# Four decoder stages on one core: the first step of self-attention prepared inside cross-attention

## The reference

```python
x = layernorm(x + attn(x))     # gated linear recurrence: sigmoid gates, associative scan, rms norm
x = layernorm(x + xattn(x, ctx_2048))
x = layernorm(x + ffn(x))
```

```python
q = rmsnorm(x @ Wq.T); k = rmsnorm(context @ Wk.T); v = context @ Wv.T
out = softmax(q @ k.T * 16 ** -0.5) @ v
```

```python
h = rms(x, w_ln1)
q, k, v = h @ wq + bq, h @ wk + bk, h @ wv + bv
q, k = rope(q, k)
x = x + softmax(causal(q @ k.T * 32 ** -0.5)) @ v @ wo
h = rms(x, w_ln2)
x = x + routed(h) + shared(h)
```

## Time and profile before

| | |
|---|---|
| median of 3 runs | 2638.78 us (2637.13 to 2641.35) |
| profiled execution, its own time | 2640.4 us |
| its span | 2638.7 us |
| granted TensorE clock, mean | 0.972 |
| TensorE busy | 2423.2 us (92%) |
| VectorE, ScalarE, GpSimd busy | 1349.4, 1362.4, 903.0 us |
| instructions | 39037 |

### The profile page before, as it was taken

One profiled execution on the slowest core, in us unless ns is written; L12 is line 12 of the kernel. 1 busy time (PEld: TensorE's weight loads), 2 busy tenths in 40 slices (PEclk: granted clock), 3 DMA queues, 4 the chain that ended last, 5 costly groups with the idle time before them and its releaser, 6 DMA issues. The chain is left out here.

```text
span 2638.7 us, 39037 instructions
## 1 busy us (share of the span) xinstructions
PE 2423.2 (92%) x15376; PEld 1558.5 (59%) x15376; DVE 1349.4 (51%) x2098; ACT 1362.4 (52%) x1731; POOL 903.0 (34%) x589
## 2 busy tenths in 40 slices
PE   7996989999999999999995899998899999999997
PEld 5885644444444444444224565655578888888786
DVE  5566534434443434343005555555655566665775
ACT  4221467666776777667993443433422355555221
POOL 1224654555455536554003333332040111111220
PEclk9997999999999999999996999999999999999999
DMA  5002675576547573855426100001162366665330
GB/s 175 17 1 82 195 201 139 133 198 172 130 121 208 150 173 83 226 153 135 113 55 212 44 1 9 9 17 51 60 203 98 102 238 207 236 211 173 124 126 34
DMA packets 207429, 330.91 MB, mean 125 GB/s; under 512 B 70992, under 2 KB 125520, under 8 KB 207056
## 3 DMA queue, kind: packets, MB, share of 16 engines
q1 hardware_dynamic: 190032, 256.46, 34.4%
q0 software_dynamic: 15056, 68.03, 7.8%
q10 hardware_dynamic: 2160, 3.93, 0.5%
HBM read 241.00 MB, written 99.42 MB: 129 GB/s over the span
## 5 line engine op out<-in xcount | busy, mean ns | idle before, releaser
L880 ACT ACTIVATE A_c_prob<-c_psum 128x1024 f32<-128x1024 f32 x832 | 786.8, 1030 | 290.6 <-PE c_psum L1083 282.3
L826 POOL TENSOR_TENSOR c_rr<-c_ms,c_half 128x32 f32<-128x32 f32 (+1 forms) x72 | 372.5, 5177 | 436.5 <-DVE c_ms L897 436.5
L1092 PE MATMUL c_psum<-A_c_prob,c_vq 128*17 128x512 f32 x3328 | 419.0, 604 | 11.2 <-DVE c_oT L1003 9.7
L1083 PE MATMUL c_psum<-c_qq,c_kq 64*128 64x512 f32 x1664 | 293.3, 441 | 27.2 <-ACT A_c_prob L880 15.4
L134 PE MATMUL c_psum<-R_c_w,S_c_c 128*128 128x512 f32 x1248 | 314.3, 401 | 0.9 <-DVE S_c_t L960 0.5
L134 PEld LDWEIGHTS c_psum<-R_c_w,S_c_c 128*128 128x128 f32 x1248 | 228.4, 189 | 123.7 <-issue 43.1
L1083 PEld LDWEIGHTS c_psum<-c_qq,c_kq 64*128 64x128 f32 x1664 | 138.2, 186 | 186.7 <-ACT A_c_prob L880 107.7
L134 PE MATMUL m_psum<-R_m_t,m_up_hi 128*128 128x256 f32 (+1 forms) x1104 | 203.5, 285 | 23.9 <-DVE R_m_t L2241 23.9
L2286 PE MATMUL m_psum<-A_m_dn_hi,A_m_a 128*128 128x512 f32 (+1 forms) x628 | 206.3, 398 | 10.7 <-DVE A_m_a L2095 10.7
L937 DVE COPY c_raw<-c_psum 128x256 f32<-128x256 f32 x89 | 37.8, 425 | 332.2 <-PE c_psum L134 332.2
L1530 DVE TENSOR_REDUCE s_topx<-s_psum 128x4 f32<-128x2048 f32 (+1 forms) x64 | 95.5, 1493 | 178.1 <-PE s_psum L1642 178.1
(11 more groups left out here) (279 smaller groups left out, 4361.6 us busy)
## 6 DMA issues: line engine op xcount, KB each, us to landing
c_kq<-kd SPq DMA_DIRECT2D x248, 208.0 KB, 5.9
kd<-S_c_t SPq DMA_DIRECT2D x96, 256.0 KB, 3.5
A_c_raw<-in_ctxT SPq DMA_DIRECT2D x89, 256.0 KB, 4.8
qd<-A_c_q SPq DMA_DIRECT2D x64, 256.0 KB
c_qq<-qd SPq DMA_DIRECT2D x64, 256.0 KB, 3.2
vd<-c_vt SPq DMA_DIRECT2D x104, 136.0 KB, 3.0
c_vq<-vd SPq DMA_DIRECT2D x31, 442.0 KB, 9.2
R_m_hs<-slots SPq DMA_DIRECT2D x23, 512.0 KB, 7.4
```

Of the source, the lines that this page charges most:

```text
L826: pool.tensor_tensor(rr[:, unit % RB, 0:n], ms[:, unit % RB, 0:n], half[:, 0:n], ALU.pow).then_inc(s_r, 1)
L880: act.activation(prob[:, t % PB, 2 * (u % 2):2 * (u % 2) + 2, :], score_banks[u % 3], ACT.Exp, scale=XD ** -0.5).then_inc(s_ex, 1)
L1083: mm = pe.matmul(score_banks[u % 3][:, s, :], kq[rows, q % 2, u % 2, kt * P:(kt + 1) * P], qq[rows, q % 2, u % 2, :], start=True, stop=True)
L1092: mm = pe.matmul(o_bank[32 * j:32 * j + VW, :], vq[:, q % 2, kt, j, :], prob[:, t % PB, j, :], start=kt == 0, stop=kt == CT - 1)
```

## The change

A fourth region Q (2 units) is added. It takes cross-attention's `raw` and `c_raw`, later the query and key parts `qk_hi` and `qk_lo` of self-attention, and `dn_raw`, `dn_lo` and `work` of the experts' stage. Cross-attention's `vt` moves into region A, and its `on` into `sq`.

The planner gets twelve more items, H0 to H3 (turns of batch 0 for self-attention) and A0 to A7 (the four quarters of the query projection of step 0, then of the key projection, three matmuls each). They are placed in blocks with one weighted sum, not before 14 blocks after the last projection. By these rules they stand in blocks 243, 245, 247, 249 (H) and 251, 253, 255, 257, 259, 261, 263, 265 (A). While a projection is between its quarters no O may be placed: O28 moves from block 253 to 258 and O29 from 261 to 266.

In block 234 (`line.ahead`) SP issues the loads of wq, wk, wv, w1 and bqk, ahead of quad 28's loads in block 235; in block 244 cosine and sine. GpSimd casts the three weights to their high parts, VectorE squares the rows of batch 0, makes the low parts and scales the rows; VectorE and GpSimd also empty the H items and rotate and split step 0's queries and keys. ScalarE does nothing of it. Self-attention then starts with its five small loads, the load of wo and the slots, and with the first maxima; A(1,0), A(1,1), V0 and V1 are placed behind one of the four maxima each.

```diff
@@ class Timeline
+    QUARTERS = 4
+        later = [("H", i) for i in range(KC)] + [("A", i) for i in range(2 * self.QUARTERS)]
-            o_ready = quads and quads[0][1] <= k - 1
+            half_way = later and later[0][0] == "A" and later[0][1] % self.QUARTERS
+            o_ready = quads and quads[0][1] <= k - 1 and not half_way
+            elif later and not turns and not heavy and len(ready) < 2 and k >= max(unit_done.values()) + 14:
+                got = later.pop(0)
+        self.ahead = put_at["T", B * self.UPB - 1] + 2
@@ cross_attention, SP
+                if k == line.ahead:
+                    sp.wait_ge(s_put, last_turn.index + 1)
+                    for i in range(3):
+                        sp.wait_ge(s_vst[i], 16 * sum(1 for n in range(2 * B * CT) if v_buf(n) == i))
+                    for c in range(KC):
+                        sp.wait_ge(s_qst[c], 16 * 4 * B)
+                    for i, name in enumerate(("wq", "wk", "wv")):
+                        sp.dma_start(staged[i], d[name].rearrange("(k p) n -> p k n", p=P)).then_inc(s_stage[i], 16)
+                    sp.dma_start(w1[:], d["w1"]).then_inc(s_small, 16)
+                    sp.dma_start(bqk[:], d["bqk"]).then_inc(s_small, 16)
+                if k == line.ahead + 10:
+                    sp.wait_ge(s_slo, 3)
+                    sp.dma_start(cos, d["cos"]).then_inc(s_angle, 16)
+                    sp.dma_start(sin, d["sin"]).then_inc(s_angle, 16)
@@ cross_attention, GpSimd
+                if piece is last_turn:
+                    pool.wait_ge(s_put, last_products.index + 1)
+                    for i in range(3):
+                        pool.wait_ge(s_stage[i], 16)
+                        pool.tensor_copy(sw_hi[i], staged[i]).then_inc(s_shi, 1)
+                    pool.wait_ge(s_sms, 1)
+                    pool.tensor_tensor(srr[:], sms[:], half[:, 0:TT], ALU.pow).then_inc(s_srr, 1)
+                if piece.kind == "A" and piece.i % line.QUARTERS == line.QUARTERS - 1:
+                    i = piece.i // line.QUARTERS
+                    pool.wait_ge(s_angle, 32)
+                    pool.tensor_tensor(rot[:, i], qk[:, i], cos, ALU.mult).then_inc(s_cos, 1)
+                    pool.tensor_tensor(rot[:, i], rot[:, i], shuffled[:, i], ALU.add).then_inc(s_rot, 1)
+                    pool.tensor_copy(qk_hi[:, 0, i], rot[:, i]).then_inc(s_qkhi, 1)
+                    pool.tensor_tensor(qk_lo[:, 0, i], rot[:, i], qk_hi[:, 0, i], ALU.subtract).then_inc(s_qklo, 1)
...
@@ cross_attention, VectorE
+                    dve.wait_ge(s_xo, i + 1)
+                if piece.kind == "H":
+                    dve.wait_ge(s_small, 32)
+                    dve.tensor_scalar(h_hi[:, i, :], src[:], w1[:, i:i + 1], None, ALU.mult).then_inc(s_hhi, 1)
+                    dve.scalar_tensor_tensor(h_lo[:, i, :], src[:], w1[:, i:i + 1], h_hi[:, i, :], ALU.mult, ALU.subtract).then_inc(s_hlo, 1)
+                if piece.kind == "A" and i % line.QUARTERS == line.QUARTERS - 1:
+                    i //= line.QUARTERS
+                    dve.tensor_scalar(qk[:, i], src[:], bqk[:, i, 0:1], None, ALU.add).then_inc(s_qb, 1)
+                    dve.stream_shuffle(shuffled[:, i], qk[:, i], [(x + SD // 2) % SD for x in range(SD)]).then_inc(s_turned, 1)
+                    dve.tensor_tensor(shuffled[:, i], shuffled[:, i], sin, ALU.mult).then_inc(s_sin, 1)
...
+            def self_attention_ahead(j):
+                if 0 <= j < TT:
+                    own.done(dve.tensor_tensor(sq[:], X[:, j], X[:, j], ALU.mult))
+                    dve.tensor_reduce(ss[:, j:j + 1], sq[:], AX_X, ALU.add).then_inc(s_ss, 1)
+                if j == TT - 1:
+                    dve.tensor_scalar(sms[:], ss[:], 1.0 / H, 1e-6, ALU.mult, ALU.add).then_inc(s_sms, 1)
+                if 4 <= j < 7:
+                    dve.wait_ge(s_shi, j - 3)
+                    dve.tensor_tensor(sw_lo[j - 4], staged[j - 4], sw_hi[j - 4], ALU.subtract).then_inc(s_slo, 1)
+                if 7 <= j < 9:
+                    dve.wait_ge(s_srr, 1)
+                    for t in (2 * j - 14, 2 * j - 13):
+                        dve.tensor_scalar(xs[:, t], X[:, t], srr[:, t:t + 1], None, ALU.mult).then_inc(s_xs, 1)
...
+                self_attention_ahead(k - line.ahead)
@@ cross_attention, TensorE
+                if piece.kind == "H":
+                    pe.wait_ge(s_xs, TT)
+                    for t in range(TT):
+                        mm = pe.transpose(dst[:, t * P:(t + 1) * P], xs[:, t, i * P:(i + 1) * P], ident[:])
+                if piece.kind == "A":
+                    i, part = divmod(i, line.QUARTERS)
+                    pe.wait_ge(s_slo, i + 1)
+                    pe.wait_ge(s_hlo, KC)
+                    mm = product3(pe, dst[:], lambda _: sw_hi[i][:, part, 0:P], lambda _: sw_lo[i][:, part, 0:P],
+                                  lambda _: h_hi[:, part, :], lambda _: h_lo[:, part, :], 1, first=part == 0, last=part == KC - 1)
@@ class Steps
-        self.start = [self.item("H", 0, k) for k in range(KC)] + [self.item("A", n, i) for n in range(2) for i in range(2)]
+        self.start = [self.item("A", 1, i) for i in range(2)]
@@ self_attention, SP
-            for i in range(4):
-                if i == 3:
-                    sp.wait_ge(s_wlo, 3)
-                sp.dma_start(w_raw[i], d[names[i]].rearrange("(k p) n -> p k n", p=P)).then_inc(s_w[i], 16)
-                if i == 0:
-                    for dst, src in ((w1, "w1"), (bqk, "bqk"), (bv, "bv"), (cos, "cos"), (sin, "sin")):
-                        sp.dma_start(dst[:], d[src]).then_inc(s_ld, 16)
+            for dst, src in ((bqk, "bqk"), (sin, "sin"), (cos, "cos"), (w1, "w1"), (bv, "bv")):
+                sp.dma_start(dst[:], d[src]).then_inc(s_ld, 16)
+            sp.dma_start(wo_raw, d["wo"].rearrange("(k p) n -> p k n", p=P)).then_inc(s_w, 16)
@@ self_attention, VectorE
             dve.wait_ge(s_ld, 80)
...
             for t in reversed(range(TT)):
                 maximum(0, t)
-            low_weights(5)
+                if t >= 2:
+                    take(line.start[TT - 1 - t])
+            dve.wait_ge(s_whi, 1)
+            dve.tensor_tensor(w_lo[3], wo_raw, w_hi[3], ALU.subtract).then_inc(s_wlo, 1)
@@ self_attention, TensorE
-            for item in line.start:
-                put(item)
-            pe.wait_ge(s_hi, 2)
             for t in reversed(range(TT)):
                 if t < TT - 1:
                     pe.wait_ge(s_top, TT - 1 - t)
                 maxima(0, t)
-                if t >= 2:
-                    put(line.values[TT - 1 - t])
+                put((line.start + line.values)[TT - 1 - t])
             put(line.turn[0])
@@ program
-        regions = [Region(nc, m, name, n * KC * H) for name, n in (("R", 6), ("S", 2), ("A", 6))]
+        regions = [Region(nc, m, name, n * KC * H) for name, n in (("R", 6), ("S", 2), ("A", 6), ("Q", 2))]
```

More of the change, by code:

```diff
@@ L628, in softmax @@
             k += 1
-        assert not heavy and not turns and not xs
+        assert not heavy and not turns and not xs and not later
+        self.ahead = put_at["T", B * self.UPB - 1] + 2
         for h in range(1, 2 * B):
@@ L1205, in find, with self_attention @@
         return next(x for x in self.items if (x.kind, x.n, x.i) == (kind, n, i))
-def self_attention(nc, X, regions, ahead, hx, slots, ident, ident16, d):
+def self_attention(nc, X, regions, first, ahead, hx, slots, ident, ident16, d):
     HPC = P // SD
@@ L1409, in high_output @@
                 act.activation(a_hi[:, n % RING, :], a[:], ACT.Identity, bias=bv[:, n % KC:n % KC + 1]).then_inc(s_ahi, 1)
-            squares("H", 0, range(TT))
-            normalise("H", 0, range(TT))
-            high_weights(0)
             act.wait_ge(s_ld, 80)
-            for item in line.start[:KC]:
+            for item in line.start:
                 take(item)
-            for part in (1, 2, 3):
-                high_weights(part)
-            for item in line.start[KC:]:
-                take(item)
-            for part in (4, 5):
-                high_weights(part)
+            act.wait_ge(s_w, 16)
+            act.activation(w_hi[3], wo_raw, ACT.Copy).then_inc(s_whi, 1)
             for item in line.values:
@@ L2337, in program @@
             slots = nc.dram_tensor("slots", (SLOTS, H), F32).ap()
-            self_attention(nc, X, regions, ahead, hx, slots, ident, ident16, d)
+            self_attention(nc, X, regions, first, ahead, hx, slots, ident, ident16, d)
         if stop_after > 3:
```

150 lines of the change are left out of this document (82 added, 68 removed).

## The result

The changed kernel takes 2610.97 us (median of 4 runs, 2605.78 to 2617.23), the kernel before beside it 2638.31 us: ratio 0.9896, interval 0.9871 to 0.9921. Run twice more it took 2611.78 and 2611.87 us. The forecast was 2611 us with a range of 2605 to 2620.

The account below looks back on a forecast made before the run. The prediction took the uncovered serial start of self-attention, at a low clock, as the bound. Terms 27.3 + 2.8 - 1.4 - 0.3 = 28.4, taken as 28, gave 2611 us, range 2605 to 2620.

Parts of the forecast that it names:

- The border: Start of self-attention: first load to first scores falls from 48.3 us to about 21, saving 27.3 us.
- fills: Start of self-attention: VectorE's small fills end at 1.8 us, so TensorE starts at 2.0 us.
- A(1,0) at the low level: Start of self-attention: this projection's 12 matmuls take 5.2 us at the 1.2 GHz level.
- The reduction: Start of self-attention: VectorE's first reduction, 2.28 us, waits for five small loads landing 4.4 to 7.0 us in; 7.0 taken.
- The output weights' low part: Start of self-attention: VectorE's 2.3 us of work ends near 20 us in, before the first exponential, so it is covered.
- Step 0: Self-attention's first step runs at the higher clock, saving 2.8 us, bounds 0 and 3.
- The second rival: Start of self-attention stays a chain at the low clock: gain 18 us, time 2621 us; chance 0.12.
- The tail: End of cross-attention: added items cost 0 in one-sum blocks, two moved output turns 0.71 us each; 1.4 us, bounds 0 and 9.8.
- The moved loads: Cross-attention: weights ahead of quad 28's loads, which land by 1278.5 to 1280, needed at 1282.2; price 0, 2 to 4 us spare.
- The splits: Cross-attention: casts, subtractions and scaling of batch 0's rows end by about 1281, before their first turn after 1284; price 0.
- The sum: Whole kernel: 27.3 + 2.8 - 1.4 - 0.3 = 28.4 us gained, taken as 28.
- the clearing: Cross-attention's end: about twenty more semaphores are cleared, costing 0 to 1 us, taken as 0.3.

Follow-up runs that it names:

- Experiments 1: Changed kernel with batch 0's turns and step 0's projections put back in self-attention's start, only weights and scaled rows moved; 2624.91 us, ratio 0.9952.
- 2: Changed kernel with only step 0's two projections and their rotation put back in self-attention's start; 2620.58 us, ratio 0.9933.
- Experiment 3: Changed kernel with the twelve added items placed in blocks with two weighted sums instead of one; 2616.25 us, ratio 0.9928.
- experiment 5: Changed kernel with the three weights loaded behind quad 28's loads instead of ahead of them; 2615.59 us, ratio 0.9918.
- 8: Changed kernel with late output turns only in one-sum blocks and 30 idle matmuls behind the last output turn; 2602.97 us, ratio 0.9860.
- 7: Changed kernel with 30 idle matmuls of 512 columns behind cross-attention's last output turn; 2609.57 us, ratio 0.9897.
- 4: Changed kernel with two more 1 MB loads, feeding nothing, ahead of quad 28's loads; 2611.75 us, run again 2610.23 us.
- experiment 6: Changed kernel with output turns, too, only in one-sum blocks in cross-attention's tail; 2607.36 us, run again 2605.76 us.

## Why the prediction was right

**The border.** Forecast 48.3 to 21, measured 48.3 to 19.9. The steps came out as priced: fills at 2.0 us, A(1,0) at the low level 4.9 us for 5.2, the items at the full level 2.8 to 3.0. The reduction was taken at the upper end of its bounds (7.0) and came at 5.2, so the second maxima followed A(1,0) without a gap; that is the microsecond by which the start is shorter than forecast. The output weights' low part ended at 1416.0 and nothing waited for it. Experiments 1 and 2 divide the 28.4 us: 12.4 for weights and scaled rows, 8.7 for the turns, 7.3 for the projections.

**Step 0.** Forecast 2.8 us. Turn to turn it takes 25.95 us (1415.16 to 1441.11), where it took 28.66: 2.7. The second rival, a start that stays at the low level, did not come about: the level rose 5.1 us behind the first maxima, and from 1402.9 us to the second turn of maxima at 1441.1 it was 1.00.

**The tail.** Forecast 1.4, measured 1.3, and at the places named: nothing in single-sum blocks, 0.60 and 0.47 us behind the two moved output turns, with two small breaks of 0.16 and 0.15 beside them. Experiment 3 is the other end: the same items in two-sum blocks make the tail 8.9 us longer than before the change, near the upper bound of 9.8.

**The moved loads.** Price 0 as forecast, but here one step was wrong: when quad 28's loads are needed. The prediction said 1282.2, the time of ScalarE's first exponential of the quad, 27.4 us into the run of 30. What needs them first is TensorE's scores for it: in the kernel with more loads TensorE begins to wait at 1273.1, 25.4 us into that run (it starts at 1247.78 there), and in the changed kernel's trace they stand at 1279.4, 25.9 us into it. So they come 1.5 to 2.0 us earlier than the prediction had them. The landing itself must be compared from the same point, because the changed kernel's run starts at 1253.58 and that of before, on which the forecast was made, at 1254.83. The loads landed 24.9 us into the run (1278.5); in the other two traces it was 24.8 and 24.4. The forecast of 1278.5 to 1280 is 23.7 to 25.2. So they came near its late end, and the margin was 0.4 to 0.9 us and not 2 to 4. The price of 0 held, but with far less to spare than the argument said: that part is luck as much as forecast.

**The splits.** The last weight landed at 1266.5 us (1256.21 + 10.3), which is 1267.8 counted as before, so as forecast. The rows were ready at 1278.2, counted as before 1279.4, and not 1281: the casts took 1.9 to 2.0 us, not the 2.45 scaled up from the context tiles, and the root ran beside the subtractions. Where the two engines overlap, the squares show it: 0.68 us alone, 1.54 beside one cast and 2.17 beside another. The Trainium skill, "SBUF — State Buffer", section "SBUF: two separate sides", calls the shared ports an exclusive lock on which the loser fully blocks. The trace agrees: both squares end 0.5 us behind the end of the cast that ran when they started, which is nearly their own length. In experiment 5 a subtraction of 2.29 us alone took 3.95 us and ended 2.1 us behind the cast that it met. The prediction read the 3.35 us of the earlier trace rows as a subtraction that is stretched and not stopped. GpSimd's timeline of the same trace says otherwise:

```profile
1424.78 3.38 POOL L1343 TENSOR_TENSOR s_qk_lo<-s_rot,s_qk_hi 128x512 fp32r<-128x512 f32 x2
1428.12 3.32 POOL L1322 TENSOR_TENSOR s_rot<-s_qk,s_cos 128x512 f32<-128x512 f32 x1
```

The subtraction started at 1426.96, GpSimd's operation ended at 1428.16, and the subtraction ended 2.15 us behind it, again nearly its own length (2.28); GpSimd's next product, 1.30 us alone, then took 3.32. By the rule the prediction had 20 us from the first cast to the rows. They took 17.2 (1260.93 to 1278.16), because the casts were shorter, the first square stood ahead of them, and the root cost nothing of its own.

**The sum.** Measured terms: 28.4 + 2.7 - 1.3 = 29.8, less 0.3 us by which the block's end takes longer (forecast as the clearing; the traces show the length, 11.35 and 11.62 us from the last exponential to the first load, and not its cause), less 0.5 us that the forecast counts twice: the turn that is quicker at the full level is in the border and in step 0. That makes 29.0. The profiled execution shows them up to the second turn, which stands 30.3 us earlier than before (1471.41, now 1441.11), 1.25 of it because the tail itself began earlier. It doesn't keep them. The last turn of maxima is 28.6 us earlier (1844.00 to 1815.41), the experts' first load 23.8 us (1891.82 to 1868.04). So 6.5 us are lost behind the second turn, 4.8 of them behind the last, in code that the change doesn't touch. The windows of before, and then of the changed kernel: first from 1420 to 1600 us, where before's still holds the end of the old start, then from the last turn of maxima to the experts' first load, which is the same work in both:

```profile
1420.00:1600.00 180.00, 158.51 (x1421) 101.97 (x1419) 99.86 (x101) 69.61 (x91) 72.80 (x63) 0.93 0.22 74
...
1844.00:1891.82 47.82, 37.31 (x292) 25.32 (x292) 26.02 (x35) 23.27 (x39) 2.03 (x3) 1.00 0.12 45
```

```profile
1420.00:1600.00 180.00, 164.77 (x1568) 104.55 (x1568) 100.15 (x107) 70.32 (x96) 63.38 (x58) 0.97 0.10 33
...
1815.40:1868.00 52.60, 43.12 (x292) 29.86 (x292) 26.31 (x35) 23.60 (x39) 2.02 (x2) 0.87 0.11 41
```

The granted clock in this last part is 0.87 instead of 1.00, and it takes 52.6 us instead of 47.8. The prediction had no term for this. In the other two traces that stretch takes 52.6 and 51.0 us. There the fifteen steps ahead of it take 396.5 us, where they took 401.25 before and 400.25 in the first trace: 4.8 us less, of which step 0 is 2.7. So 2 us of gain in the middle stand against 3 to 5 us of loss at the end, and the medians, 27.3, 28.3 and 25.7 us under before, lie around 29.0 less 1 to 3. The forecast of 28 is in the same place, partly because these terms, which it didn't have, nearly cancel.

## What to carry to other kernels

Work that stands alone at a stage's border can be laid into the slack of the stage before it, and what that costs is decided by the block that it lands in: here 0 us beside one weighted sum and 0.5 to 1.1 us beside two. For a load that is pushed back, look for its first reader on every engine; here it was the engine that feeds the one on the critical path, and it came 1.5 to 2 us earlier. When you check a forecast of moments against a new trace, count both from the same event, since the whole trace can be shifted. Before moving items into the gaps, see what they push out of them: two output turns cost 1.3 us, and choosing their blocks too took the tail under its old length.

## What the runs showed of the chip

- **One program's executions differ by 10 us and more, and their granted clocks differ with them.** Three traces of the changed kernel begin self-attention at 1395.83, 1390.45 and 1394.95. They agree up to 324.5 us (the third load of a quad's values, 324.50 and 324.47 in the first two) and part in the next two quads (the loads at 403.77 and 399.06). The window of the first trace, then that of the second:

```profile
375.00:425.00 50.00, 44.05 (x262) 21.79 (x264) 18.75 (x36) 28.57 (x30) 20.19 (x10) 0.93 0.49 136
```

```profile
375.00:425.00 50.00, 45.88 (x298) 21.93 (x298) 21.36 (x41) 34.00 (x36) 25.02 (x10) 1.00 0.49 136
```

  At 0.93 ScalarE gets through 30 exponentials and small operations, at 1.00 through 36. The third trace has 0.93 there too, and is late too. Up to the run of 30 exponentials the thirteen traces of the changed kernel and of its variants hold the same work. The four with 1.00 in this window (one of them of the changed kernel) start that run at 1246.6 to 1249.6 us, the nine with 0.93 to 0.97 at 1249.5 to 1256.0. So this window is one of the places where the executions part, ahead of self-attention, where the expectation had looked for them, and there are others. By how much a median of 4 to 6 such runs can be off was not measured; the three of the changed kernel lie 0.9 us apart, from executions that spread over 7 to 14 us.
- **At self-attention's end the clock falls in most traces, and the length of that stretch goes with it.** From the last turn of maxima to the experts' first load every kernel here does the same work. The granted clock and the time are 1.00 and 47.8 us before the change and in experiments 3 and 8; 0.96 and 48.2 in experiment 5; 0.93 and 50.4 to 50.5 in experiments 1, 2 and 7 and in the second traces of 4 and 6; 0.90 and 51.0 in the first traces of 4 and 6 and in the third of the changed kernel; 0.87 and 52.6 in its first two. The kernels of experiments 1 and 2 keep a part of the old start and fall all the same, those of 3 and 8 don't keep it and stay up. What makes the clock fall there was not tested.
- **Ten microseconds of idling cost TensorE 3 to 5 us at the low level.** In the changed kernel's first trace it was 5.1 us, from 1397.8 to 1402.9, in its other two 4.6 and 4.8, and in the two of experiment 6, behind the same 10.9 us of idling, some 3.1 and 4.2 (read from the spacing of the matmuls, 0.43 us and then 0.23). With 7.1 us of idle matmuls and 4.1 us of idling ahead of it, the level still fell behind the first maxima, and was back some 3.8 us behind their start, which is inside that range.
